# Two-layer FFT block: the first box row's sum on TensorE, and the image statistics in another form

## What is computed

```
def _gn(v, G=8, eps=1e-5):            # mean and variance over 2 channels x 512 x 512
    ...
    return ((g - m) / jnp.sqrt(s + eps)).reshape(v.shape)

# layer 0: rfft2, a 3x3 complex convolution over the spectrum, irfft2
x = x + _L0_conv_ref(_gn(x), L0_conv_w_real, L0_conv_w_imag, L0_conv_b_real, L0_conv_b_imag)
# layer 1: 15 x 15 box mean with zero padding
x = x + _L1_conv_ref(_gn(x))
```

## Time and profile before

| | us |
|---|---|
| median of 3 runs | 3428.91 |
| lowest, highest | 3428.09, 3434.28 |
| the profiled execution, its run time | 3430.94 |
| its span, first to last instruction | 3428.9 |
| granted TensorE clock, mean | 0.983 of full |
| busy share: PE, DVE, POOL, ACT | 90%, 90%, 79%, 71% |

### The profile page before, as it was taken

The page is one execution under the profiler, slowest core; times in us unless marked ns, Lnnn a source line. Parts: engine busy times, 40 slices in busy tenths (PEclk is TensorE's granted clock), DMA queues, the critical chain, the costliest instruction groups (busy, mean ns, idle before and its releaser), DMA issues.

```text
span 3428.9 us, 112515 instructions
## 1 busy us (share of the span) xinstructions
PE 3076.5 (90%) x36064; PEld 1864.6 (54%) x36064; DVE 3076.0 (90%) x6018; ACT 2448.6 (71%) x4742; POOL 2714.2 (79%) x2231
## 2 busy tenths in 40 slices
PE   2189989999889998999899998999989999899986
PEld 1155555555555555555565555555555555555555
DVE  7789989999889989899898998989988998989987
ACT  2568865788658876588666886578865787658876
POOL 5069975899749987599876997589974998759986
PEclk9599999999999999999999999999999999999999
DMA  8656678666876659776696666966687666876655
GB/s 209 203 86 129 128 209 263 115 126 125 251 209 127 128 130 278 178 127 128 154 301 135 128 128 196 276 111 128 123 241 225 121 127 141 258 186 130 128 136 169
DMA packets 725102, 573.58 MB, mean 167 GB/s; under 512 B 591776, under 2 KB 667136, under 8 KB 710400
## 3 DMA queue, kind: packets, MB, share of 16 engines
q1 hardware_dynamic: 702336, 451.67, 56.5%
q10 hardware_dynamic: 22400, 117.46, 13.3%
HBM read 262.08 MB, written 148.90 MB: 120 GB/s over the span
## 4 chain that ended last, share of the span: by engine, by line
PE 46%; DVE 16%; issue 14%; POOL 11%; SPq 5%; DMA 4%; ACT 2%; ACTq 1%; DVEq 1%; POOLq 0%
PE p L621 21%; PE h_ps L531 8%; PE h_odd L531 7%; DVE ob_all L1350 5%; SPq L420 3%; PE p L765 3%; DMA out<-ob_all 2%; PE h_ps L621 2%; POOL g_more L1489 2%; POOL biases L1489 2%; PE p L628 2%; POOL xT_more L1489 2%; DVE stat L1103 1%; POOL ob_all L1432 1%; DVE bd_all L1342 1%
## 5 line engine op out<-in xcount | busy, mean ns | idle before, releaser
L621 PE MATMUL p<-arena,bd_all 64*64 64x512 f16 x16896 | 1264.3, 380 | 25.8 <-DVE ob_all L1265 14.0
L621 PEld LDWEIGHTS p<-arena,bd_all 64*64 64x64 f16 x16896 | 557.4, 105 | 435.7 <-issue 281.8
L1429 POOL TENSOR_TENSOR ob_all<-ob_all,img 128x512 f32<-128x512 f32 x512 | 664.2, 1297 | 63.7 <-DVE ob_all L1265 59.4
L1432 POOL TENSOR_TENSOR ob_all<-ob_all 128x512 f32<-128x512 f32 x512 | 654.3, 1278 | 40.2
L884 ACT ACTIVATE img<-img,half_row (+1 forms) x1024 | 489.0, 531 | 5.0 <-ACT half_row L874 0.4
L1265 DVE SCALAR_TENSOR_TENSOR ob_all<-p,biases,cosw 128x256 f32<-128x256 f32 x1024 | 445.5, 476 | 24.8 <-PE p L621 11.8
L1422 POOL TENSOR_TENSOR arena<-arena 128x512 f16<-128x512 f32 x256 | 309.1, 1208 | 172.6 <-ACT arena L858 172.6
L1271 DVE SCALAR_TENSOR_TENSOR ob_all<-p,biases,cosw 128x256 f32<-128x256 f32 x1024 | 443.4, 474 | 0.0
L857 ACT ACTIVATE arena<-img,sc 128x512 f16 (+1 forms) x512 | 434.9, 849 | 0.0
L1283 DVE BATCH_NORM_STATS2 stat<-img (+1 forms) x512 | 355.5, 694 | 58.5
L1350 DVE SCALAR_TENSOR_TENSOR ob_all<-p,img 128x512 f32<-128x512 f32 x512 | 346.7, 677 | 58.9 <-PE p L765 39.5
(11 more groups left out here) (213 smaller groups left out, 5588.5 us busy)
## 6 DMA issues: line engine op xcount, KB each, us to landing
out<-ob_all SPq DMA_DIRECT2D x512, 256.0 KB, 4.7
bd_all<-bd_dram SPq DMA_DIRECT2D x512, 224.0 KB, 2.5
img<-in_x ACTq DMA_DIRECT2D x168, 512.0 KB, 7.0
img<-in_x ACTq DMA_DIRECT2D x112, 256.0 KB, 5.2
img<-in_x SPq DMA_DIRECT2D x24, 512.0 KB, 25.3
arena<-img SPq DMA_DIRECT2D x24, 448.0 KB, 4.4
bd_dram<-ob_all SPq DMA_DIRECT2D x11, 768.0 KB, 3.6
arena<-arena SPq DMA_TRANSPOSE x512, 2.7
```

Of the source, the lines that this page charges most:

```text
L621: m = mm(bank[out_half * HP:(out_half + 1) * HP, :], bd[s % RB][rows, 6 * lm + (j if own else j + 1), :], part, start=opens and i3 == 0, s ...
L1429: G.tensor_tensor(q, term_row[s % 2][0], parity(img[:, t, :]), ALU.add).then_inc(first_added, 1)
L1432: G.tensor_tensor(q, q, term_row[s % 2][1], ALU.add).then_inc(q_done, 1)
```

## The change

1. **Row 0's sum.** POOL's `presum`, `tail` as a sum, its scaling on DVE (L1355) and the signal `tail_ready` are gone. TensorE makes the sum in the bank `h_odd`, unscaled: `head` with `ident` and the seven rows T-7 to T-1 with `prev`, 8 fp32 products of 512 columns that stand where `keep_warm` products stood. `group_mean` comes ahead of the product of row T-2 and `group_variance` ahead of that of row T-1. ACT reads `h_odd` and writes the scaled `head`. `turn_first` is 4 transposes of `head`.
2. **POOL's differences** wait for `s_mean` in place of `tail_ready`.
3. **ACT** makes `edge_bias` (3 columns, in place of DVE's L1144 to L1146) after `s_scale`, then `head`; `high_part(0)` stands ahead of `scale_row(2)`.
4. **Statistics.** One `bn_stats` over the 128 means, a `tensor_reduce` that sums the 128 sums of squares, `bn_aggr` over 6 numbers, and one operation after `s_mean` that joins the two.
5. **Operations on `sc`.** Three-operand operations of DVE (scalar_tensor_tensor) on one column become `tensor_scalar` with pointers to two columns or one. Four operations at the end are gone (two of them unused since).
6. **The correction of the means** is split: rows 0 to 59 between the last two `finish_row`, rows 60 to 63 behind them.

```diff
+                pe.wait_ge(presummed, b + 1)
+                pe.sem_inc(warm_step, 1)
+                mm(h_odd[:], tb["ident"][:], head, start=True, stop=False)
+                for t in range(T - R, T):
+                    if t == T - 2:
+                        group_mean(b * 2 + 2)
+                    if t == T - 1:
+                        group_variance(b * 2 + 2)
+                    pe.wait_ge(x1_whole, b * T + t + 1)
+                    pe.sem_inc(warm_step, 1)
+                    m = mm(h_odd[:], tb["prev"][:], img[:, t, :], start=False, stop=t == T - 1)
+                m.then_inc(head_summed, 1)
+                keep_warm(p2[:], 4)
...
-                        cols = slice(k * P, (k + 1) * P)
-                        mm(turned_ps[0][:, k, :], head[:, cols], tb["ident"][:], start=True, stop=False)
-                        m = mm(turned_ps[0][:, k, :], tail[:, cols], tb["prev"][:], start=False, stop=True)
+                        m = nc.tensor.transpose(turned_ps[0][:, k, :], head[:, k * P:(k + 1) * P], tb["ident"][:])
...
+                flat_stat = stat[:].rearrange("p t s -> p (t s)")
+                V.bn_stats(sc[:, 28:34], flat_stat[:, 1:6 * T:3])
+                lk(V.tensor_reduce(sc[:, 34:35], flat_stat[:, 2:6 * T:3], mybir.AxisListType.X, ALU.add))
                 V.memset(sc[:, 19:20], 0.0)
-                V.bn_aggr(sc[:, 0:2], stat[:].rearrange("p t s -> p (t s)")).then_inc(s_mean, 1)
+                V.bn_aggr(sc[:, 0:2], sc[:, 28:34]).then_inc(s_mean, 1)
+                dve.wait_ge(s_mean, n)
+                lk(V.scalar_tensor_tensor(sc[:, 1:2], sc[:, 34:35], 1.0 / (2 * T * HALF), sc[:, 1:2], ALU.mult, ALU.add))
...
-                lk(V.scalar_tensor_tensor(sc[:, 11:12], sc[:, 7:8], sc[:, 7:8], sc[:, 4:5], ALU.mult, ALU.mult))
+                lk(V.tensor_scalar(sc[:, 11:12], sc[:, 7:8], sc[:, 7:8], sc[:, 4:5], ALU.mult, ALU.mult))
...
-                pool.wait_ge(tail_ready, b + 1)
+                pool.wait_ge(s_mean, b * 2 + 2)
```

More of the change, by code:

```diff
@@ L231, in build @@
         vwrap = sb("vwrap", [P, 3, 2])
[L232 removed]
+        edge_bias = sb("edge_bias", [P, 3])
         edge = sb("edge", [P, 8])
@@ L955, in high_part @@
                     copy(parts[u % 3][:, 0], turned_ps[u % NTURN]).then_inc(high_done, 1)
-                act.wait_ge(presummed, b * 2 + 2)
-                scaled(head, head, sc[:, 10:11], sc[:, 18:19]).then_inc(head_ready, 1)
+                scaled(edge_bias[:], tb["ends"][:], sc[:, 9:10]).then_inc(edge_made, 1)
+                act.wait_ge(edge_made, b + 1)
+                act.wait_ge(head_summed, b + 1)
+                scaled(head, h_odd[:], sc[:, 10:11], edge_bias[:, 2:3]).then_inc(head_ready, 1)
                 scale_row(1)
+                high_part(0)
                 scale_row(2)
-                high_part(0)
                 def load_next(t, rows, signal):
@@ L1351, in add_box @@
                                            ALU.mult, ALU.add).then_inc(row_out, 1)
-                dve.wait_ge(presummed, b * 2 + 2)
-                dve.wait_ge(s_scale, b * 2 + 2)
-                V.tensor_scalar(tail, tail, sc[:, 10:11], sc[:, 23:24], ALU.mult, ALU.add).then_inc(tail_ready, 1)
                 low_part(0)
```

74 lines of the change are left out of this document (22 added, 52 removed).

## The result

| | before | changed |
|---|---|---|
| median of 4 runs each, us | 3428.50 | 3390.01 |
| lowest, highest, us | 3426.83, 3434.28 | 3389.12, 3392.79 |
| profiled execution: span, us | 3428.9 | 3390.6 |
| granted TensorE clock, mean | 0.983 | 0.984 |

The ratio is 0.9887, 95% interval 0.9871 to 0.9903: 1.1% faster. The forecast was 3387.6 us with a range of 3381 to 3404.

The account below looks back on a forecast made before the run. Engines waiting for each other one at a time, from layer 0's last row to layer 1's first output row, bound the kernel. 5.02 us per image, 40.2 in eight, -1.5 clock, +0.4 input: -41.3, to 3387.6 us, range 3381 to 3404.

Parts of the forecast that it names:

- A: End of layer 0: without POOL's sum, POOL's last-row additions and DVE's last L1280 start earlier, -1.60 us per image.
- B: Last correction of the means, only 8 elements left before the aggregation: -0.53 us per image.
- C: Aggregation of x1's statistics: short operations and bn_aggr over 6 numbers replace 1.88 us, -1.16 us per image.
- D: From s_mean to s_scale: operations dropped at the end, against slower ones with pointers, -0.12 us per image.
- E: From s_scale to layer 1's first output row: POOL's differences start early, ACT alone sets the start, -1.61 us per image.
- The clock: Around x1's group mean in four images: new products avoid TensorE's idle time and reduced clock, -1.5 us per launch.
- The input: Input statistics: TensorE's queue holds the group mean, aggregation gain lost in seven images, slower operations cost 0.19; +0.4 per launch.
- R5: Rival, layer 1: transfers pace the stage from a fixed time, so the gain is given back, 3424 us; 3%.
- R1: Rival, the port race at s_mean: POOL starts first and the joining operation waits out its subtraction, +6.8, 3394.4 us; 10%.
- R2: Rival, statistics to s_scale: one-column tensor_scalar operations stop beside POOL too, +15.7 in all, 3413.2 us; 9%.
- R3: Rival, aggregation: bn_aggr's price is fixed, so the new aggregation is a loss, +13.6, 3401 us; 8%.
- R4: Rival, ahead of the group mean: TensorE at reduced clock under the six products, slower than before, 3437 us; 4%.

Follow-up runs that it names:

- old_aggr: Changed kernel with the one bn_aggr over 384 numbers put back in both statistics, joining operation gone: 3403.16 us, ratio 0.9928 to the kernel before.
- pe_more: Changed kernel with three more fp32 products of 512 columns on TensorE ahead of the eight, result overwritten: 3400.15 us, ratio 0.9924 to the kernel before.
- act_order: Changed kernel with ACT's old order, scale_row(2) ahead of high_part(0): 3397.74 us, one run.
- aggr_alone: Kernel before with only the new form of the aggregation and its joining operation: 3425.78 us, ratio 0.9996 to the kernel before.
- presum_back: Changed kernel with POOL's old sum of rows 57 to 63 put back as unread work: 3421.46 us, ratio 0.9975 to the kernel before.
- input_order: Changed kernel with the input's group mean, three warming products and group variance put ahead of the four Hilbert products: 3388.49 us, one run.
- further3: Changed kernel with ACT's old order, `head` bias on DVE, input statistics reordered and three-operand again, L502's product ahead of four warming products: 3375.46 us, ratio 0.984.
- two_inputs: Changed kernel with four one-column statistics operations back as scalar_tensor_tensor with two SBUF inputs: 3408.14 us, ratio 0.9936 to the kernel before.

## Where the prediction held, point by point

Per image, from the first image's rows and the table:

| step | forecast | measured |
|---|---|---|
| A, POOL out of the way | -1.60 | -1.74 |
| B, last correction | -0.53 | -0.54 |
| C, aggregation | -1.16 | -1.11 (`old_aggr`: 1.13) |
| D, `s_mean` to `s_scale` | -0.12 | -0.07 |
| E, `s_scale` to the first output row | -1.61 | -1.43 |
| sum | -5.02 | -4.89 |

The sum is right to 0.13 us because the two largest misses, A and E, point opposite ways. **A** was 0.14 short. POOL started 0.07 us behind its term (440.70 against 439.75 + 0.88), where 0.16 had been taken. DVE started the last L1281 0.07 us behind POOL's end (442.08 + 1.27, L1435), where it was 0.03 before: the correction of 120 elements held it up by 0.04 us, not 0.12, though it took 0.82 us, stopped beside POOL's addition. Against that POOL's two additions took 0.03 us longer. **B** and **C** came as worked out: 0.21 us from the last correction to the aggregation, 0.77 from there to its end (forecast 0.22 and 0.72); that `bn_aggr` over 6 numbers takes just the 0.18 us assumed could not be known from a row. The Trainium skill (VectorE: DVE Perf Modes, Rules for kernel authors) wants the number of chained DVE operations small; the rows and `old_aggr` speak against it here, since one operation of 1.88 us lost to four that take 0.77.

**TensorE** kept up with 0.41 us to spare, forecast 0.7: six products took 446.05 - 440.64 = 5.4 us and not 5.1. `pe_more` confirms the margin.

**D**: from the second group product to `s_scale` 2.08 us pass, 0.15 less than before, a little more than the 0.12 forecast. The other 0.08 lies ahead of that product, where DVE's copy came 0.49 us behind the start of the first group product (446.95 against 446.46) and not 0.41, as before:

```profile
454.73 0.38 PE L494 MATMUL p<-sc,group_mean 128*128 128x1 f32 x2 [1.06 <-DVE sc L1121]
...
455.14 0.16 DVE L1124 COPY sc<-p 128x1 f32<-128x1 f32 x1 [0.48 <-PE p L494]
```

**E**, the largest miss, 0.18 (0.21 by its own steps, which add up to 4.88 us and so to a gain of 1.64, not 1.61): the term "the four transposes of `head` are just done" failed. They begin only when `head` is scaled and end at 451.66, so part 0 starts 1.96 us behind `s_scale` and not 1.72. `act_order` shows the same 0.23 from the other side. The three-column operation cost 0.30 us for 0.20. What followed kept the assumed pace: the first output row stands 0.64 us behind part 1, forecast 0.63.

**The clock.** The stage to the group mean summed to 39.2 us before against 8 x 4.72 at full clock: 1.4 us for the reduced clock, forecast 1.5, and all eight are equal now. The 0.6 of the earlier trace rows is a mean: the window holds a stretch at 0.5, the 1.2 GHz level, and one at 1.00. And the prediction's reason is half of the matter. In all eight images of the kernel before TensorE idled 2.36 to 2.40 us ahead of the `keep_warm` products that stand before the group mean, and the clock fell in four. It fell in four of eight behind 2.34 to 2.39 us in `aggr_alone`, in seven of eight behind 2.49 to 2.65 us in `presum_back`, in two of eight behind 1.5 us in `old_aggr`, and around the group products in no image where TensorE idled 0.6 us or less ahead of them. What decides between two images with the same idle time is open. **The input.** From the last output row to the product L502 it was 13.61 us before and 13.38 and 13.81 in the two traces of the changed kernel: the forecast +0.19 lies inside that spread. From the start of the input's aggregation to L502 the medians of seven images are 5.39 us before and 5.51 and 5.45 after, 0.06 to 0.12 more, so C's gain is lost here, as forecast. The prediction had named TensorE's queue as what holds the group mean: from the start of the aggregation to it 2.32 us pass before, 2.44 and 2.38 after, and 1.35 in `input_order`, which moves it up in the queue. `further3` shows the same for L502.

**The sum.** The three stages at the seam gave 13.9 + 26.4 = 40.3 us, forecast 41.7; the medians differ by 38.5. The rest is less than the spread of the stages that no edit touches. The stage from the first to the last output row (seven images) was 802.8 us in one trace of the changed kernel and 794.4 in the other, and 796.3 to 801.0 in those of the eight kernels of the first two sets; before has 794.7. So **R5**, gain given back in layer 1, which the first trace alone would have suggested with +8.1 us, is out. A part of the 8 us goes with the clock: five of the seven images of the first trace hold a stretch at the 1.2 GHz level in this stage, one in the second trace, none in that of the kernel before. Over all fourteen traces the stage takes 114.6 us on average in the 36 images with such a stretch and 113.6 in the 62 without. What brings these stretches about, and the rest of the variation, is open.

**The other rivals.** **R1**: the race never takes place. POOL is not released by `s_mean` but by the copies of its first rows, 1.27 us later (the idle mark "<-DMA" on L1474 above), 0.4 to 1.5 us later over the images of both traces. The prediction missed that wait, and had E's picture of POOL "3 us ahead" wrong by as much; it cost nothing, since ACT wants the first difference only at 450.78. By the rows DVE would have been first anyway: in `old_aggr`, where the copies are there first, POOL starts 0.17 us behind `s_mean` (seven of eight images), and in the changed kernel the joining operation starts 0.03 us behind it (446.44 against 446.41). But the stop that R1 feared is real: `presum_back` and `aggr_alone` show it on this very operation, 1.09 and 0.93 us. **R2**: out; all one-column `tensor_scalar` beside POOL took 0.15 to 0.27 us, while `two_inputs` shows the stop for two arrays. This is the rule of the Trainium skill (SBUF - State Buffer, Who interferes with whom), that a DVE operation with at most one SBUF input, outside the two-port modes, does not contend with GpSimd; the traces agree down to one element. **R3**: out, `bn_aggr` over 6 numbers takes 0.18 us. **R4**: out for the changed kernel, but `presum_back` shows its mechanism in seven of eight images: 2.05 us per product at a granted 0.51, behind 2.5 us of idle TensorE.

## What to carry to other kernels

Where engines wait for each other one at a time, the edits are not additive: the new aggregation alone brought nothing measurable, and 1.13 us per image once POOL's sum was gone; so try them together and then take each away. Before an engine is let start earlier, look at what the others do beside it: here one-column operations with two SBUF arrays had to become ones with pointers first, or 2.0 us per image of the gain were lost. Warming products belong behind the last product that somebody waits for, not ahead of it; in `further3` the mean granted clock stayed at 0.986.

## What the runs showed of the hardware beyond that

- A DVE operation of a single column with two arrays in SBUF, started during a POOL operation, ends when that ends: 0.16 us became 1.09, 0.93, 1.00 and 1.19 us. Where POOL's operation had only 0.1 us left, it took 0.22 us, as alone (the first of the three in `two_inputs`, 0.22 to 0.39 us over the images). Wider ones do the same: the correction of 120 elements began at 442.71 in the changed kernel and at 442.12 in `presum_back`, and ended at 443.53 and 443.37, both times 0.18 to 0.19 us behind the end of POOL's operation.
- `bn_aggr` took 1.88 us for 384 numbers and 0.18 for 6; `bn_stats` over 128 strided elements 0.33, `tensor_reduce` over as many 0.30.
- A `tensor_scalar` on one column took 0.15 us with constants, 0.21 with one pointer, 0.27 with two.
- ACT's operation on 3 columns (L943) took 0.30 us, its square root on one column 0.20.
